# Rope on the feed-forward attention: products read from PSUM, the sine product swapped and subtracted, plain fp32 scores, V's bias added after the values

## What is computed

```python
q = (h @ wq + bq).reshape(b, s, H, HD).transpose(0, 2, 1, 3)
k = (h @ wk + bk)...; v = (h @ wv + bv)...
q = q * cos + _rotate_half(q) * sin      # _rotate_half(x) = concat(-x2, x1)
k = k * cos + _rotate_half(k) * sin
scores = einsum('bhqd,bhkd->bhqk', q, k) / sqrt(HD)   # causal mask
probs = softmax(scores)
out = einsum('bhqk,bhkd->bhqd', probs, v)
return out.reshape(b, s, H * HD) @ wo + bo
```

## Time and profile before

| | |
|---|---|
| median of three runs | 551.22 us (550.22 to 552.91) |
| profiled execution, span | 548.8 us, 11087 instructions |
| TensorE (matmul) | busy 86% of the span |
| VectorE | 81% |
| GpSimd | 58% |
| ScalarE | 56% |
| mean granted TensorE clock | 0.974 |

### The profile page before, as it was taken

The page is one execution under the profiler, slowest core; times in us unless marked ns, Lnnn a source line. Parts: engine busy times, 40 slices in busy tenths (PEclk is TensorE's granted clock), DMA queues, the critical chain, the costliest instruction groups (busy, mean ns, idle before and its releaser), DMA issues.

```text
span 548.8 us, 11087 instructions
## 1 busy us (share of the span) xinstructions
PE 470.7 (86%) x3380; PEld 424.1 (77%) x3380; DVE 446.4 (81%) x1215; ACT 306.9 (56%) x821; POOL 319.2 (58%) x362
## 2 busy tenths in 40 slices
PE   0379999989867999999989999889989997679996
PEld 0269998889755788888879889878879796569896
DVE  5857677876489999989989999989989999963644
ACT  2148777676325666656656567557556565463341
POOL 7952707801245958949848768758767663151352
PEclk9999999999978999999998999999989999997899
DMA  8000000220112342243333242252242330000011
GB/s 288 2 2 2 1 2 2 78 78 2 39 39 59 76 114 67 55 133 76 76 96 76 66 131 69 59 134 57 65 126 57 76 77 2 1 2 0 1 40 38
DMA packets 17962, 32.46 MB, mean 59 GB/s; under 512 B 3972, under 2 KB 6152, under 8 KB 17800
## 3 DMA queue, kind: packets, MB, share of 16 engines
q1 hardware_dynamic: 14008, 23.35, 16.0%
q10 hardware_dynamic: 3920, 8.69, 5.7%
HBM read 14.20 MB, written 1.05 MB: 28 GB/s over the span
## 4 chain that ended last, share of the span: by engine, by line
DVE 31%; PE 27%; issue 22%; POOL 9%; ACT 6%; DMA 3%; DVEq 1%; ACTq 1%; POOLq 0%; SPq 0%
PE bank L1220 9%; DVE room L875 6%; PE bank L1173 5%; POOL split_room L245 4%; PE bank L1156 3%; DVE room L869 3%; DVE PR L995 3%; DVE o_parts L939 3%; DVE sm L950 2%; POOL qk_room L423 2%; DVE V L881 2%; DVE yacc L986 2%; ACT PR L519 2%; DMA qk_room<-qk_room 2%; DVE PR L994 1%
## 5 line engine op out<-in xcount | busy, mean ns | idle before, releaser
L423 POOL TENSOR_TENSOR qk_room<-qk_room,cst_sb 128x512 f32<-128x512 f32 x64 | 88.5, 1383 | 49.9 <-DMA qk_room<-qk_room 49.9
L570 ACT ACTIVATE PR<-sm,nm 128x128 f32<-128x128 f32 (+1 forms) x128 | 57.3, 448 | 93.7 <-DVE nm L950 93.7
L245 POOL TENSOR_TENSOR split_room<-room,split_room 128x256 fp32r<-128x256 f32 (+1 forms) x60 | 72.0, 1201 | 19.6 <-ACT split_room L550 19.6
L1220 PE MATMUL bank<-hH,qk_parts 128*128 128x512 f32 x256 | 83.2, 407 | 0.0
L875 DVE TENSOR_TENSOR room<-room,qk_room 128x512 f32<-128x512 f32 x64 | 67.2, 1050 | 10.8 <-POOL qk_room L423 10.8
L869 DVE TENSOR_TENSOR room<-qk_room,cst_sb 128x512 f32<-128x512 f32 x64 | 58.6, 916 | 0.0
L1220 PEld LDWEIGHTS bank<-hH,qk_parts 128*128 128x128 f32 x256 | 50.4, 197 | 9.2
L544 ACT ACTIVATE qk_room<-bank,qk_bias 128x512 f32<-128x512 f32 x64 | 43.5, 680 | 22.0 <-DVE room L875 21.5
L1220 PE MATMUL bank<-hL,qk_parts 128*128 128x512 f32 x128 | 53.0, 414 | 3.0 <-issue 1.8
L519 ACT ACTIVATE PR<-bank,nxm 128x128 f32<-128x128 f32 (+1 forms) x128 | 45.8, 434 | 16.1 <-DVE nxm L837 11.9
L1173 PE MATMUL bank<-PTs,room 128*128 128x128 f32 x384 | 50.7, 275 | 0.1
(11 more groups left out here) (201 smaller groups left out, 1398.1 us busy)
## 6 DMA issues: line engine op xcount, KB each, us to landing
qk_room<-qk_room SPq DMA_DIRECT2D x128, 128.0 KB, 2.4
stg<-in_wqkv ACTq DMA_DIRECT2D x6, 768.0 KB, 5.5
stge<-in_we ACTq DMA_DIRECT2D x7, 256.0 KB, 3.1
stg<-in_wqkv SPq DMA_DIRECT2D x2, 768.0 KB, 6.3
stgo<-in_wo ACTq DMA_DIRECT2D x6, 256.0 KB, 3.0
x_sb<-in_x SPq DMA_DIRECT2D x4, 256.0 KB, 6.2
bv_sb<-in_bv SPq DMA_DIRECT2D x1, 1024.0 KB, 4.8
out_y<-yacc SPq DMA_DIRECT2D x4, 256.0 KB, 2.1
```

Source lines behind the costliest of these rows:

```text
L245: eng.tensor_tensor(low, v, high.bitcast(F32), ALU.subtract).then_inc(s["split_low"], 1)
L423: pool.tensor_tensor(v, v, cst_sb[:, col:col + 256].unsqueeze(1).to_broadcast([P, 2, 256]), ALU.mult).then_inc(s["chunk_sw"], 1)
L570: ins = act.activation(PR[:, q, a:e], sm[:, q, a:e], ACT.Exp, bias=nm[:, q, t:t + 1], scale=-1.0, accum_out=rs[:, q, t:t + 1])
L1220: ins = pe.matmul(outp, l, r, start=(m == 0), stop=(m == n - 1))
```

## The change

- `chunk_out` on ScalarE and `qk_f` go. VectorE makes both rope products itself, straight from the projected chunk in PSUM: `scalar_tensor_tensor` adds the bias (`qk_bias`, one value per partition) and multiplies with the table. The sine product goes to `qk_t` right after the maxima, the cosine product to `QT` after the normalisation.
- SyncE swaps the sine product instead of the chunk.
- GpSimd subtracts the swapped sine product from `QT` (`rope_add`), instead of multiplying with the sine table. VectorE's addition goes.
- The split of the roped chunks (`roped_high`, `roped_low`, `q_split`, `k_split`) goes; both products of `scores` are plain fp32, and wait for `rope_done`.
- V leaves PSUM without a bias, on ScalarE instead of VectorE. Its bias is added per partition to the transposed output: in the rounding to `oH` (ScalarE) and in `o_low` (VectorE). GpSimd copies the two values of a pair to `bv_pair`. The 1 MB load of the bias rows ahead of the loop goes, and a small load `bv_cols` stands among the first ones.
- Semaphores follow: VectorE's `rope_sin` waits for `chunk_pe` and, as guard, `rope_done`; TensorE's guard of the projection is `chunk_cos` instead of `chunk_f`; ScalarE waits for `chunk_pe` ahead of the rounding of the next weights.
- Ahead of the loop, chunks 0 to 3 are roped by VectorE between the parts of the last batch's residual and norm (`rope(0)` to `rope(3)`).

```diff
@@ SyncE
+            sp.dma_start(bv_cols[:, :], bv.rearrange("o (h d) -> d (o h)", d=HD), ...).then_inc(s["d_bv"], 16)
-            sp.wait_ge(s["m6_pe"], m6["Q", B - 1, 1, 1] + 1)
-            sp.dma_start(bv_sb[:, :], bv.to_broadcast([P, H * HD])).then_inc(s["d_bv"], 16)
             def swap(n, q):
-                sp.wait_ge(s["chunk_f"], n + 1)
-                sp.dma_start(qk_sw[0:64, q, :], qk_f[64:128, q, :]).then_inc(s[f"d_sw{q}"], 16)
-                sp.dma_start(qk_sw[64:128, q, :], qk_f[0:64, q, :]).then_inc(s[f"d_sw{q}"], 16)
+                sp.wait_ge(s["chunk_sin"], n + 1)
+                sp.dma_start(qk_sw[0:64, q, :], qk_t[64:128, q, :]).then_inc(s[f"d_sw{q}"], 16)
+                sp.dma_start(qk_sw[64:128, q, :], qk_t[0:64, q, :]).then_inc(s[f"d_sw{q}"], 16)
@@ GpSimd
-            def rope_sin(sw_count, q, k):
+            def rope_add(n, sw_count, q, c, g):
+                pool.wait_ge(s["chunk_cos"], n + 1)
                 pool.wait_ge(s[f"d_sw{q}"], sw_count)
-                col = C_RSINK if k else C_RSINQ
-                v = qk_sw[:, q, :].rearrange("p (b t) -> p b t", b=2)
-                pool.tensor_tensor(v, v, cst_sb[:, col:col + 256]..., ALU.mult).then_inc(s["chunk_sw"], 1)
+                v = QT[:, c, 512 * g:512 * (g + 1)]
+                pool.tensor_tensor(v, v, qk_sw[:, q, :], ALU.subtract).then_inc(s["rope_done"], 1)
...
+                if j == 1 and not (isinstance(i, int) and (i == 0 or i >= NP)):
+                    head_biases(i, 0)
+                if j == 3 and not (isinstance(i, int) and i >= NP):
+                    if isinstance(i, int) and i == NP - 1:
+                        pool.wait_ge(s["b_oL"], U * i)
+                    head_biases(i, 1)
-                if unit(i, j, -4):
-                    roped_low(pool, U * i + j + 4, j % 4, (j + 4) // 4 % 2)
@@ ScalarE
-                if unit(i, j, -LEAD):
-                    if 2 <= j < 6:
-                        act.wait_ge(s["wqk_bias"], 4 * (i + 1) + j - 2 + 1)
-                    chunk_out(T + LEAD, q, chunk_at(j)[0], True)
-                elif unit(i, j, -4):
-                    roped_high(T + 4, j % 4, (j + 4) // 4 % 2)
...
-                    act.activation(oH[...], bank[3][:, 0:256], ACT.Copy).then_inc(s["b_oH"], 1)
-                if unit(i, j, -LEAD):
-                    roped_high(U * i + j + 4, j % 4, (j + 4) // 4 % 2)
+                    act.activation(oH[...], bank[3][:, 0:256], ACT.Identity, bias=head_bias(j)).then_inc(s["b_oH"], 1)
+                m = (j + 2) // 2
+                if j % 2 == 0 and (not isinstance(i, int) or (2 < B * i + m < B * NP)):
+                    v_out(B * i + m, m % B)
...
+                    act.wait_ge(s["chunk_pe"], U * i + j + 5)
@@ VectorE
+            def rope_part(out, q, c, col):
+                return dve.scalar_tensor_tensor(out..., O_B[q][:, :]..., qk_bias[:, c:c + 1], cst_sb[:, col:col + 256]..., ALU.add, ALU.mult)
+            def rope_sin(n, q, c, guard):
+                dve.wait_ge(s["chunk_pe"], n + 1)
+                if guard:
+                    dve.wait_ge(s["rope_done"], n - 1)
+                rope_part(qk_t[:, q, :], q, c, C_RSINK if c % 2 else C_RSINQ).then_inc(s["chunk_sin"], 1)
+            def rope_cos(q, c, cols_):
+                rope_part(QT[:, c, cols_], q, c, C_RCOSK if c % 2 else C_RCOSQ).then_inc(s["chunk_cos"], 1)
...
-                if unit(i, j, -4):
-                    rope_add(T + 4, q, j % 4, groups[(j + 4) // 4 % 2])
+                if unit(i, j, -LEAD):
+                    if 2 <= j < 6:
+                        dve.wait_ge(s["wqk_bias"], 4 * (i + 1) + j - 2 + 1)
+                    rope_sin(T + LEAD, q, c, True)
...
-                    v_out(B * i + m, m % B, i + m // B)
...
-                dve.tensor_tensor(oL[...], bank[3][:, 0:256], h.bitcast(F32), ALU.subtract).then_inc(s["b_oL"], 1)
+                dve.scalar_tensor_tensor(oL[...], bank[3][:, 0:256], head_bias(j), h.bitcast(F32), ALU.add, ALU.subtract).then_inc(s["b_oL"], 1)
@@ TensorE
             def project_qk(n, q, c, g, guard):
                 if guard:
-                    pe.wait_ge(s["chunk_f"], n - 1)
+                    pe.wait_ge(s["chunk_cos"], n - 1)
...
-                pe.wait_ge(s["split_low"], U * i + 4 * (j // 4) + 2 * r + 2)
+                pe.wait_ge(s["rope_done"], U * i + 4 * (j // 4) + 2 * r + 2)
...
-                three(S_B[j % 2][:, P:3 * P], [([q_split[...]...], [k_split[...]...])]).then_inc(s["b_s"], 1)
+                pe.matmul(S_B[j % 2][:, P:3 * P], QT[:, 2 * r, second], QT[:, 2 * r + 1, both], start=True, stop=True).then_inc(s["b_s"], 1)
```

More of the change, by code:

```diff
@@ L87, in build_kernel @@
         qk_room = sb("qk_room", [P, 4, 512])
[L88 removed]
+        qk_t = qk_room[:, 0:2, :]
         qk_sw = qk_room[:, 2:4, :]
@@ L232, in pt_copy, with head_bias @@
             copy(PTs[:, p % 2, :], PT_B[p % 2][:, :]).then_inc(s[copier(p)[0]], 1)
[L234 to L245 removed]
+        def head_bias(j):
+            return bv_pair[:, 0 if j >= 2 else 1, j % 2:j % 2 + 1]
         h2T = qk_room[:, :, :].rearrange("p a n -> p (a n)").rearrange("p (k n) -> p k n", k=KT)
@@ L537, in _, with v_out @@
             o_evac(B - 1)
[L539 to L558 removed]
+            def v_out(m, b):
+                act.wait_ge(s["v_pe"], m + 1)
+                act.activation(V[:, 2 * b:2 * b + 2, :].rearrange("p t n -> p (t n)"), bank[6][:, :], ACT.Copy).then_inc(s["v_ready"], 1)
+            v_out(0, 0)
+            v_out(1, 1)
+            h_high(B - 1)
+            v_out(2, 2)
             def step(i, j):
@@ L897, in _ @@
-            rope_cos(2, 0, 2, groups[0])
-            roped_low(dve, 0, 0, 0)
-            roped_low(dve, 1, 1, 0)
-            rope_add(2, 0, 2, groups[0])
-            v_out(2, 2, 0)
-            rope_cos(3, 1, 3, groups[0])
-            roped_low(dve, 2, 2, 0)
-            rope_add(3, 1, 3, groups[0])
+            rope(2)
+            rope(3)
             def second_norm(b, phase, batches=1):
@@ L954, in _ @@
             maxima(0, 0)
-            roped_low(dve, 3, 3, 0)
             for n in range(4, LEAD):
-                rope_cos(n, n % 2, n % 4, groups[1])
+                rope(n)
             dve.wait_ge(s["yacc_init"], B)
```

104 lines of the change are left out of this document (34 added, 70 removed).

## The result

The changed kernel took 524.88 us in the median of four runs (523.37 to 525.54); the kernel before, beside it, 551.34 (550.22 to 552.91). The ratio is 0.9527, with a 95% interval of 0.9482 to 0.9572: 26 us less. Forecast were 527.0, within 518 to 540. The profiled execution took 523.37 us, with a span of 521.5.

A forecast was written before the change was run, and what follows sets the result against it. TensorE was taken to set a 4.37 us floor, with GpSimd and VectorE pushing it off. Loop -25.5, remaining waits +4, end -2.5 made -24 us: 527 us from 551.22, range 518 to 540.

The forecast's parts named there:

- The one certain loss of the sum: TensorE's scores: a plain fp32 product replacing three fast ones costs 0.08 us more per step, floor 4.45 us.
- what remains of waits, +4: Loop: about one TensorE wait of 0.6 us per eight steps at low_o or o_low, +4 us in all.
- The two rope products at 0.74 us without spread: VectorE in the loop: both products read from PSUM always take 0.74 us, as their sign of being right.
- A step of at most 4.07 us: VectorE in the loop: mean step 4.07 us at most, under TensorE's 4.45, so VectorE leaves the path.
- The excess of the normalisation: VectorE's L994 and L995, still exposed to GpSimd: 0.6 us per step above their undisturbed times.
- The new waits: VectorE's sine product waits for the same step's projection and for GpSimd's subtraction of the chunk two before.
- the ring: Sine product, swap, subtraction, next sine product but one: must fit two steps, 8.9 us; slower than before from a 7.7 us landing.
- about 1 us: Slack of VectorE's o_low before TensorE needs it; fails only when GpSimd blocks L994 and L995 for their full length.
- Start and end: Ahead of the loop between 2.5 us earlier and later, taken as 0; at the end -2.5 us.
- VectorE as the bound of the changed kernel: Rival: new products held up beside GpSimd, or projection wait shifts VectorE; 4.7 us steps, 537 us (532 to 543); chance 0.15.
- The ring with GpSimd: Rival: sine, swap, subtraction loop exceeds two steps, 5.1 us per step, 561 us, slower than before; chance 0.07.
- No change for the bound: Rival: TensorE's idle time only moves to the new waits, plain product adds 4.6 us; 553 us; chance 0.06.

The follow-up runs named there:

- e2: Changed kernel with the split put back (ScalarE rounds, GpSimd makes low halves, three fast products, scores wait for split_low): 530.17 us, ratio 0.9574.
- e4: Changed kernel with ScalarE's chunk_out put back, both rope products reading that copy from SBUF: 576.61 us, ratio 1.0406.
- e7: Changed kernel with one more GpSimd pass over 512 columns per step, between the swap's landing and the subtraction: 532.36 us, ratio 0.9668.
- e9: Kernel before with the weight load at j = 6 cut from 768 to 256 KB, q and k weights not renewed: 540.47 us, ratio 0.9801.
- e8: Kernel before with V copied out of PSUM by ScalarE inside the loop, V's bias left out: 556.76 us, ratio 1.0107.
- e1: Kernel before with only the split of the roped chunks removed, both score products plain fp32, rope unchanged: 525.14 us, ratio 0.9499.
- e3: Changed kernel with the subtraction of the swapped sine product on VectorE, after the maxima, instead of GpSimd: 526.28 us, ratio 0.9533.
- e11: The run with both rope products from ScalarE's SBUF copy, sine product moved to after the normalisation: 563.56 us, ratio 1.0238.
- e6: Changed kernel with the second score product replaced by one fast product of zeros of the same size: 507.82 us, ratio 0.9222.

## Why the prediction was right, and where its steps were off

**The bound and the floor.** TensorE 4.37 us per step, 4.45 with the plain product: measured 4.45, and e2 gives the other side, 4.38, with the three fast products. The one certain loss of the sum, +0.08 us, is 0.07. What the prediction had wrong here is the kernel before: it read TensorE's 4.37 as what set the step there, with VectorE and GpSimd pushing it off "a few times in every eight steps". VectorE's own 4.61 us per step were already more. The forecast didn't suffer, since it priced the changed kernel's step by each engine anew.

**Loop.** Forecast 244.8 + 4 us, measured 245.6. The term that was mis-sized is "what remains of waits, +4": it was 0.8, all in the first of the 55 steps. I had kept a part of the wait for `low_o` and `o_low`. PE's longest waits from 160 to 450 us in the changed kernel (two more, of 0.7 and 0.6, are for `o_low`):

```profile
PE bank L1266 <- DVE PR L971: 3.3, 4, 1.5
PE bank L1195 <- POOL hL L401: 1.7, 1, 1.7
PE bank L1195 <- DVE room L850: 1.2, 2, 0.8
PE bank L1195 <- POOL qk_parts L361: 0.8, 1, 0.8
```

None of them lies between 185 and 420 us, where TensorE has no idle time; none is of the scores, and `low_o` is in none. The span shows these 3 us (-27.3 where -24 was taken); of the medians, -26.3 apart, 2 are left.

**VectorE.** The two rope products at 0.74 us without spread: right. A step of at most 4.07 us, waits within it included, under TensorE's 4.45: right too, VectorE is busy for 3.54. The rows of the products, and those of the normalisation (ns min/median/max):

```profile
L850 DVE SCALAR_TENSOR_TENSOR qk_room<-bank,qk_bias,cst_sb x64: 740/751/752, 150.8 to 423.0; 128x512 f32<-128x512 f32 x64
L850 DVE SCALAR_TENSOR_TENSOR room<-bank,qk_bias,cst_sb x64: 734/744/748, 151.5 to 425.4; 128x512 f32<-128x512 f32 x64
...
L970 DVE TENSOR_SCALAR PR<-PR,rs x64: 285/286/1406, 174.0 to 443.4; 128x128 f32<-128x128 f32 x64
L971 DVE TENSOR_SCALAR PR<-PR,rs x64: 339/347/1405, 174.2 to 443.6; 128x256 f32<-128x256 f32 x64
```

Against L869 and L875 the spread is gone. The excess of the normalisation, taken at 0.6 us per step from L994 and L995, was 0.17 (means of 427 and 365 ns between 185 and 420 us, over undisturbed 285 and 340): GpSimd runs a third less, and a pass meets the normalisation less often. The prediction had said "at most".

The rule of the Trainium skill that was weighed there (VectorE: DVE Perf Modes, the section on the TRN2 errata), a dearer fixed cost for a PSUM source, would by an estimate from its cycles have had the products cost some 0.13 us more per step than from SBUF. The rows of e4 and of the changed kernel differ by 0.06 us per product (694 and 751, 684 and 744 ns). But the form differs too, and L881, two operands with one in PSUM, takes 678, no more than from SBUF. So these rows speak for the form with a scalar per partition, not for PSUM, as the place of the 0.06; that form from SBUF wasn't tried.

**The new waits.** The sine product waits for the projection of the same step, 33.6 us in 51 waits of at most 0.8: as counted, and in VectorE's reserve. (Of the ring, the prediction's sum 0.74 + 6.4 + 1.28 is 8.4, not 8.5, and a landing of 7.8, not 7.7, makes two steps of 9.82; neither changes anything.) When one pass of GpSimd holds the normalisation, the slack of "about 1 us" can be seen:

```profile
303.74 1.41 DVE L970 TENSOR_SCALAR PR<-PR,rs 128x128 f32<-128x128 f32 x1
303.78 1.28 POOL L411 TENSOR_TENSOR room<-room,qk_room 128x512 f32<-128x512 f32 x1 [4.73 <-DMA qk_room<-qk_room]
...
305.99 0.47 DVE L915 SCALAR_TENSOR_TENSOR o_parts<-bank,bv_pair,o_parts 128x256 fp32r<-128x256 f32 x1
```

`o_low` ends at 306.46 and is used at 307.46. The prediction said that it fails only when both products are held for their full length; e7 is that case, and there TensorE waits 0.58 us.

**Start and end.** 0 and -2.5 were taken, -0.1 and -2.5 measured. The start is a balance, as argued: two new waits for the cosine products, against the addition and the split that are gone.

**The reason for the gain.** The prediction let VectorE leave the path because its products no longer meet GpSimd. That VectorE left the path is right; that it needs the products from PSUM is not. VectorE's time per step, hold-ups by GpSimd included, over the 48 steps from unit 5 to unit 53 (busy time of a window, by 48):

| | step, us | VectorE busy per step, us | TensorE's own work, us |
|---|---|---|---|
| kernel before | 4.92 | 4.61 | 4.37 |
| e9, without the collision | 4.69 | 4.64 | 4.37 |
| e8, V on ScalarE | 4.96 | 4.59 | 4.37 |
| e1, split gone | 4.45 | 3.91 | 4.45 |
| e2, split kept | 4.38 | 3.71 | 4.38 |
| e3, subtraction on VectorE | 4.45 | 4.02 | 4.45 |
| changed kernel | 4.45 | 3.54 | 4.45 |

The three runs in which VectorE needs more than TensorE are slow, the four in which it needs less are at TensorE's floor. e1 gets there by fewer passes of GpSimd, which hold the same instructions up less; e2 gets there by fewer operands in SBUF, with GpSimd as busy as before. Each is enough alone. That the hold-ups are the common cause is read from these rows; a run that takes them away and leaves both halves of the kernel before in place wasn't made.

Being below the floor isn't enough where VectorE stands still within the step: e4 (3.55 us busy in steps of 5.26) and e11 (4.22 in 5.02). What reading PSUM is good for at that place is that it takes ScalarE's copy, and with it the exponentials, out of the way of a sine product that stands right after the maxima (e4), and, as e11 shows, that the products stay free of the hold-ups.

**The rivals.** VectorE as the bound of the changed kernel: fell (e3, e6). The ring with GpSimd: fell, and e7 shows the margin. No change for the bound: fell.

## What to carry to other kernels

Find the step in which the leading engine has no idle time, and price the change against that floor. Compare every other engine with that floor by its busy time per step, hold-ups counted in, and not by its share of the span. Several edits that each remove lateness bring you to the floor once, not several times, so test them one by one. In an in-order queue ask of each instruction what its producer stands behind: a product moved forward is worth something only if its input doesn't come from behind the work that this engine feeds.

## What the runs showed of the hardware

- A pass of GpSimd and a VectorE product with its operands in SBUF hold each other up for whole instructions: L970, 0.29 us alone, takes 1.41 beside a pass of 1.28 that started with it (the rows above). GpSimd loses too. Its passes over 128x512 elements, 220 to 420 us, in the kernel before and in the changed one (busy us, mean ns, idle before):

```profile
L423 POOL TENSOR_TENSOR qk_room<-qk_room,cst_sb 128x512 f32<-128x512 f32 x41 | 57.6, 1404 | 29.9 <-DMA qk_room<-qk_room 29.9
```

```profile
L411 POOL TENSOR_TENSOR room<-room,qk_room 128x512 f32<-128x512 f32 x45 | 58.0, 1289 | 65.4 <-DMA qk_room<-qk_room 65.4
```

  By the Trainium skill (SBUF — State Buffer, the section "SBUF: two separate sides") the two engines share a port pair as a lock for the whole instruction, against VectorE's two-port modes and, where GpSimd's pass reads SBUF, against its operations with two SBUF inputs; these rows agree, and the products with an operand in PSUM, 734 to 752 ns in all 128, stay free of it.
- A plain fp32 product of 256 columns costs TensorE 0.07 us more than three fast ones (4.45 against 4.38 per step) and 0.32 more than one (4.45 against 4.13).
- Cutting the load of 768 KB beside the swaps to 256 gained 11 us where a chain without slack stood behind them (e9). The changed kernel has the same load and the same swaps, and TensorE has no idle time there.
